# First attention: the mask is added by TensorE, the maxima are plain reductions, and VectorE copies the second head's row of maxima

## The chip, the cores and the metric

The kernel runs on one core of a Trainium2 chip. The metric is device time in microseconds (us) of one launch. TensorE (matmuls, PE in the profile; its weight loads are PEld), VectorE (DVE), ScalarE (ACT), GpSimd (POOL) and SyncE (SP, which issues the DMAs here) each work through a list of their own, and wait for each other by semaphores.

## The reference, cut to what matters

The input is x with 4 batches of 512 rows of 256. The first layer is `x + LN(attn(LN(x)))`, the second has an attention with 16 heads of 128 and a mixture of experts. The change lies in the first attention, which has 16 heads of 16 dimensions:

```python
sim = jnp.einsum('bhsd,bhtd->bhst', q, k) * scale
causal = jnp.tril(jnp.ones((S, S), dtype=bool))
sim = jnp.where(causal[None, None], sim, -jnp.inf)
weights = jax.nn.softmax(sim, axis=-1)
out = jnp.einsum('bhst,bhtd->bhsd', weights, v)
```

## The kernel before, in words

**Stages.** The first 58 us load, normalise and project x. Then the first attention runs in `step1(s)` on TensorE, VectorE, ScalarE and GpSimd, for 32 pairs of heads, s = 0 to 31, one pair in a step; its last step ends near 229 us. After it all engines meet at a fence (`meet`), and the second attention, the shared experts, the routed experts and a last sum follow.

**One pair of heads.** Head 0 of a pair (a = 0) has its queries and keys in partitions 0 to 63 of the tile `stk`, head 1 in partitions 64 to 127. A matmul of one head uses 64 rows of the array. The scores are made twice. In the first pass (`score`, line 1610) the queries are the rows of PSUM, and only the part that the causal mask keeps is computed: for the query block n (1 to 4) 128 x 128n scores. VectorE takes the negated maximum of each row (`row_max`, `mask_and_max`, line 1135): one custom instruction that negates the scores, adds the mask and keeps the minimum, and an accumulator read that writes the result to a column of `least`. TensorE transposes `least` (line 1653, which calls `turn`, line 1574) into a bank, in which row 0 and row 64 now hold the maxima of the two heads. ScalarE copies these two rows, 1 x 512 each, to `stk` (lines 866 to 868). The second pass (`score_t`, line 1617) makes the transposed scores with this row as one more term of the sum, so that the maximum is subtracted by the matmul itself, and ScalarE takes the exponential (`exp`, line 862). GpSimd zeroes what the mask forbids there, and `values` (line 1627) multiplies by v.

**The order of a step on TensorE** (line 1604 on). It is written out by hand, and the pairs overlap: while pair s is in its second pass, pair r = s + 1 is in its first.
1. `S1_PARTS` of pair r: the scores (0, 4), (1, 4) and (0, 2), written as (head, n), in banks 0, 1 and 2. Each waits for the maxima that still use its bank, those of pair s of the "rest".
2. The transposes of `least` of pair s. They wait for all maxima of s (`a1_max`) and for the third exponential of pair s - 1, whose bank they take.
3. `values` of the first key block of pair s - 1, and in odd steps the transposes of `o1_sum`.
4. `S1_REST` of pair r: (0, 3), (1, 3), (0, 1), (1, 1), then (1, 2). (0, 3) waits for the maximum (0, 4), (1, 3) for the maximum (1, 4), and (1, 2) for the maximum (0, 2).
5. After the wait for ScalarE's copies (`a1_m`, line 1686) the first three `score_t` of pair s.
6. The other `values`, and other work by step number (the output projection in steps s % 8 = 2 takes most).
7. `score_t` (1, 2), (0, 3), (1, 3), (0, 1), (1, 1); (0, 3) and (1, 3) wait for the first and second exponential.

**VectorE** takes in a step the maxima (0, 4), (1, 4), (0, 2) of pair s + 1, in odd steps `weigh` (line 1186), then the maxima (0, 3), (0, 1), (1, 3), (1, 1), (1, 2), and at some steps the statistics and scalings of the layer's end. **ScalarE** takes the two copies, exponentials 0 and 1, in even steps a copy of `o1_sum`, then exponentials 2 to 4, and at some steps copies of the layer's end. Below a step is counted from the start of its transposes of `least` to the next such start.

The last stage (lines 1492 to 1506) takes statistics of the final sums, with a semaphore `t_st` of its own.

## Time and profile before

| | |
|---|---|
| median of 3 runs | 1226.99 us (1226.29 to 1227.85) |
| the profiled execution | 1226.03 us |
| its span in the profile | 1224.3 us |
| granted TensorE clock, mean | 0.987 of full speed |
| 32 steps of the first attention | 57.9 to about 229 us |

The profile lists instructions by engine and by the line that issued them. Its durations go from the start of an instruction to its last result, so that instructions of one engine overlap, and two that follow each other start closer together than their durations say.

### The profile page before, as it was taken

To read this page: it belongs to the slowest core of one execution; us is meant where nothing else is said; L and a number is where in the kernel's file an instruction comes from. 1 tells how busy PE (TensorE), PEld (TensorE's weight loads), DVE (VectorE), ACT (ScalarE), POOL (GpSimd) and SP (SyncE) were. 2 spreads that over 40 slices of the span, in tenths; PEclk is the share of its full clock that TensorE was granted. 3 is DMA by queue.
4 is the path that set the end of the run, shared out by engine and by line. 5 is a ranking of instruction groups with operands and counts; after the bars stand their busy time and mean duration, and the time that the engine had idled before them with its cause. 6 is when DMAs were issued, how large, how long until landed. Compare 5 with 4: busy or idle time off the path is not lost.

```text
span 1224.3 us, 25085 instructions
## 1 busy us (share of the span) xinstructions
PE 1167.3 (95%) x7980; PEld 1004.5 (82%) x7980; DVE 895.2 (73%) x2799; ACT 692.3 (57%) x1717; POOL 580.1 (47%) x844
## 2 busy tenths in 40 slices
PE   6999999899999999999999999999998889999994
PEld 5766566689999999999999999999997769999961
DVE  5777888577777777887777887778876755555555
ACT  3487888655556565556564565655566434444432
POOL 4063655454344444447353365534354446666650
PEclk9999999999999999999999999999999989999998
DMA  8965655355631121212112132111214137777776
GB/s 264 286 184 170 178 164 176 91 178 175 204 109 62 57 84 57 80 52 91 68 36 69 36 102 73 43 63 35 70 62 134 61 114 122 117 119 118 111 143 206
DMA packets 111715, 139.58 MB, mean 114 GB/s; under 512 B 11300, under 2 KB 94756, under 8 KB 111460
## 3 DMA queue, kind: packets, MB, share of 16 engines
q1 hardware_dynamic: 97140, 119.10, 32.1%
q0 software_dynamic: 14448, 18.88, 9.6%
q8 instruction: 69, 1.13, 0.4%
q14 instruction: 58, 0.48, 0.1%
HBM read 63.36 MB, written 61.87 MB: 102 GB/s over the span
## 4 chain that ended last, share of the span: by engine, by line
PE 79%; DVE 6%; ACT 3%; POOL 3%; issue 3%; DMA 3%; SPq 2%; POOLq 0%; ACTq 0%; DVEq 0%
PE bank L1513 59%; PE bank L1755 6%; PE bank L1932 4%; PE bank L1574 2%; PE bank L1627 2%; PE bank L1610 2%; PE bank L1617 1%; POOL xs_rows L704 1%; DMA sum_rows<-mid,goal 1%; POOL sum_rows L766 1%; PE bank L1911 1%; PE bank L1942 1%; SPq L393 1%; DVE bank L1135 1%; ACT pT L862 1%
## 5 line engine op out<-in xcount | busy, mean ns | idle before, releaser
L1135 DVE CUSTOM_DVE_ANT_0 bank<-bank,mask 128x512 f32<-128x512 f32 (+3 forms) x512 | 235.3, 522 | 40.4 <-PE bank L1610 20.4
L970 ACT ACTIVATE p<-bank,stat 128x512 f32<-128x512 f32 (+3 forms) x256 | 131.4, 526 | 137.9 <-issue 133.2
L557 POOL CAST w_hl<-raw_qkv 128x512 fp32r<-128x512 f32 x96 | 58.5, 610 | 313.3 <-DMA raw_qkv<-in_qkvo 159.6
L1513 PE MATMUL bank<-xT,w_hl 128*128 128x512 f32 x768 | 189.6, 395 | 0.0
L1513 PEld LDWEIGHTS bank<-xT,w_hl 128*128 128x128 f32 x768 | 144.1, 188 | 34.6
L766 POOL DMA_INDIRECT sum_rows<-mid,goal x79 | 123.1, 1559 | 75.4 <-DVE mid L1468 64.3
L1513 PE MATMUL bank<-pT,v 128*128 128x128 f32 (+3 forms) x768 | 137.3, 328 | 0.0
L1234 DVE SCALAR_TENSOR_TENSOR qk<-bank,qk 128x512 fp32r<-128x512 f32 x128 | 87.1, 688 | 66.8 <-ACT qk L910 66.5
L1513 PE MATMUL bank<-qk 128*128 128x512 f32 (+3 forms) x768 | 130.8, 320 | 3.1 <-DVE pT L1345 2.4
L1513 PEld LDWEIGHTS bank<-qk 128*128 128x128 f32 x768 | 120.6, 191 | 12.2 <-DVE v L1234 2.6
L558 POOL TENSOR_TENSOR w_hl<-raw_qkv,w_hl 128x512 fp32r<-128x512 f32 x96 | 124.0, 1292 | 7.8
L910 ACT ACTIVATE qk<-bank 128x512 fp32r<-128x512 f32 x128 | 76.1, 596 | 78.4 <-PE bank L1513 77.9
L1513 PEld LDWEIGHTS bank<-pT,v 128*128 128x128 f32 x768 | 109.7, 190 | 2.9
L1513 PE MATMUL bank<-wo_hl,o 128*128 128x256 f32 x768 | 107.6, 290 | 1.8 <-DVE o L1387 1.4
L1345 DVE TENSOR_TENSOR pT<-bank,pT 128x128 fp32r<-128x128 f32 (+3 forms) x256 | 107.0, 480 | 0.0
L1360 DVE SCALAR_TENSOR_TENSOR hs<-bank,part,hs 128x256 f32<-128x256 f32 x256 | 105.8, 474 | 1.1 <-PE bank L1513 1.1
L1513 PEld LDWEIGHTS bank<-w_hl,xT 128*128 128x128 f32 x768 | 99.3, 188 | 5.7
L1513 PE MATMUL bank<-w_hl,xT 128*128 128x256 f32 x768 | 101.1, 280 | 0.0
L1513 PE MATMUL bank<-w_hi,sh_hi 128*128 x316 | 97.5, 350 | 1.3 <-issue 1.2
L1513 PEld LDWEIGHTS bank<-wo_hl,o 128*128 128x128 f32 x768 | 95.9, 191 | 2.4 <-DVE o L1387 1.8
L862 ACT ACTIVATE pT<-bank 128x512 f32<-128x512 f32 x160 | 85.3, 604 | 19.6 <-PE bank L1617 18.2
L960 ACT ACTIVATE pT<-bank 128x128 fp32r<-128x128 f32 (+3 forms) x256 | 91.1, 453 | 0.0
(237 smaller groups left out, 2284.6 us busy)
## 6 DMA issues: line engine op xcount, KB each, us to landing
raw_qkv<-in_qkvo SPq DMA_DIRECT2D x32, 768.0 KB, 5.6
xs_rows<-blank SPq DMA_DIRECT2D x32, 520.0 KB, 3.5
xs_rows<-blank SPq DMA_DIRECT2D x5, 2730.0 KB, 14.0
xrow<-xs_rows SPq DMA_DIRECT2D x79, 130.0 KB, 2.5
raw_o<-in_qkvo SPq DMA_DIRECT2D x32, 256.0 KB, 3.8
sum_rows<-blank SPq DMA_DIRECT2D x3, 2176.0 KB, 8.5
stk<-xT SPq DMA_DIRECT2D x96, 64.0 KB
stk<-k_hl SPq DMA_DIRECT2D x96, 64.0 KB
```

Of the source, the lines that this page charges most:

```text
L558: pool.tensor_tensor(lo, raw, f32(hi), ALU.subtract).then_inc(done, 1)
L766: pool.indirect_dma_start(sum_d[sum_of(i)], bass.IndirectOffsetOnAxis(goal[:, i % NY:i % NY + 1], 0), yt[:, i % NY, :], None, compute_op=A ...
L862: act.activation(pT1[:, s % 2, i, :], st1(s, i)[:, :], ACT.Exp).then_inc(a1_exp, 1)
L910: act.activation(dst, qkv_bank(n, i)[:, :], ACT.Copy, scale=(SCALE2 if i == 0 else 1.0))\
L960: act.activation(pT2[:, HI, QOFF[kj]:QOFF[kj + 1]], bank[t][:, 0:TB - P * kj], ACT.Copy).then_inc(b_pth, 1)
L970: act.activation(p2[:, n % 2, POFF[qi]:POFF[qi + 1]], s2(t), ACT.Exp, scale=-1.0, bias=stat2[:, 0, n % 2, t:t + 1], accum_out=stat2[:, 1, ...
L1135: return dve.tensor_tensor_reduce(scores, scores, mask[:, TB - scores.shape[1]:], scale=-1.0, scalar=-2.0 * MASKED, op0=ALU.add, op1=ALU.m ...
L1234: dve.scalar_tensor_tensor(lo, qkv_bank(n, i)[:, :], SCALE2 if i == 0 else 1.0, f32(hi), ALU.mult, ALU.subtract).then_inc(b_lo, 1)
L1345: dve.tensor_tensor(pT2[:, LO, QOFF[kj]:QOFF[kj + 1]], bank[t][:, 0:TB - P * kj], f32(pT2[:, HI, QOFF[kj]:QOFF[kj + 1]]), ALU.subtract).th ...
L1360: ins = dve.scalar_tensor_tensor(own, bank[4 + c][:, D * (j - 2 * c):D * (j - 2 * c + 1)], part2[:, n % 4, TPB - 1 - j:TPB - j], own, ALU. ...
L1513: ins = pe.matmul(out, a, b, start=start and i == 0, stop=stop and i == len(pairs) - 1, **kw)
L1755: ins = pe.transpose(bank[t][:, P * (qi - kj):P * (qi - kj + 1)], p2[:, (n - 1) % 2, POFF[qi] + P * kj:POFF[qi] + P * (kj + 1)], ident[:, :])
```

## The change

The additions to the first attention are: `ident16`, an identity in bf16; `forbid`, a matmul of this identity with the mask, accumulated onto the last 128 columns of a score block (of the blocks n = 3 and n = 1 of a head together, 256 columns); and a semaphore `a1_md`. `row_max` becomes a `tensor_reduce` with the maximum, positive instead of negated, so that the row of ones in `stk` becomes a row of -1. VectorE copies row 64 to `stk` between its first maximum (0, 4) and its second (1, 4); ScalarE copies row 0 alone. The second attention keeps its custom instruction. In the last stage the semaphore `t_st` goes, and `link`, which waits for each pair of statistics, takes its place.

```diff
--- before.py
+++ after.py
@@ -87,6 +87,7 @@
         xT = sb(ctx, "xT", [P, B, 2, C, TB], F32R)
         ident = sb(ctx, "ident", [P, P])
 
+        ident16 = sb(ctx, "ident16", [P, P], BF16)
         mask = sb(ctx, "mask", [P, TB], BF16)
         ln_w = sb(ctx, "ln_w", [P, 2, C])
         gate_raw = sb(ctx, "gate_raw", [P, C, E])
@@ -216,7 +217,7 @@
 
         stk_in = [sem(f"stk_in{i}") for i in range(NSTK)]; stk_zero = sem("stk_zero")
         a1_zero = sem("a1_zero"); a1_vpad = sem("a1_vpad"); a1_s = sem("a1_s"); a1_max = sem("a1_max")
-        a1_mt = sem("a1_mt"); a1_m = sem("a1_m"); a1_st = sem("a1_st"); a1_exp = sem("a1_exp"); a1_sel = sem("a1_sel")
+        a1_mt = sem("a1_mt"); a1_m = sem("a1_m"); a1_md = sem("a1_md"); a1_st = sem("a1_st"); a1_exp = sem("a1_exp"); a1_sel = sem("a1_sel")
         a1_pv = sem("a1_pv"); a1_oe = sem("a1_oe"); a1_ot = sem("a1_ot")
         a1_xo = sem("a1_xo"); a1_xt = sem("a1_xt"); a1_o = sem("a1_o")
 
@@ -250,7 +251,7 @@
         e_h = sem("e_h"); e_ht = sem("e_ht"); e_htc = sem("e_htc"); e_dn = sem("e_dn"); e_y = sem("e_y")
         y_sent = [sem(f"y_sent{i}") for i in range(NY)]
 
-        t_in = [sem(f"t_in{i}") for i in range(2 * B)]; t_sum = sem("t_sum"); t_old = sem("t_old"); t_st = sem("t_st"); t_mean = sem("t_mean")
+        t_in = [sem(f"t_in{i}") for i in range(2 * B)]; t_sum = sem("t_sum"); t_old = sem("t_old"); t_mean = sem("t_mean")
         t_x = sem("t_x"); t_out = sem("t_out")
         stored = sem("stored")
 
@@ -505,7 +506,8 @@
                                base=0, pattern=[[-1, P]], channel_multiplier=1).then_inc(const, 1)
             pool.wait_ge(const, 4)
             pool.tensor_copy(mask[:, :], mask_f).then_inc(const, 1)
-            pool.wait_ge(const, 5)
+            pool.tensor_copy(ident16[:, :], ident[:, :]).then_inc(const, 1)
+            pool.wait_ge(const, 6)
             pool.memset(blank[:, :], 0.0).then_inc(d_blank, 1)
             pool.wait_ge(d_blank, 1)
             pool.iota(blank[:, D:D + 1].bitcast(I32), [[0, 1]], base=NOWHERE, channel_multiplier=0)\
@@ -513,7 +515,7 @@
             pool.memset(f32(stk[:, :, :, :]), 0.0).then_inc(stk_zero, 1)
             for a in range(2):
                 pool.wait_ge(stk_zero, 1 + a)
-                pool.memset(f32(stk[64 * a:64 * a + 1, :, 1, :]), 1.0).then_inc(stk_zero, 1)
+                pool.memset(f32(stk[64 * a:64 * a + 1, :, 1, :]), -1.0).then_inc(stk_zero, 1)
             pool.wait_ge(stk_zero, 3)
             pool.wait_ge(ph1_wl, 1)
             pool.tensor_tensor(qkv1_hl[:, LO, :, 2 * D:3 * D], qkv1[:, :, 2 * D:3 * D],
@@ -863,9 +865,7 @@
 
                 if s < N1:
                     act.wait_ge(a1_mt, s + 1)
-                    for a in range(2):
-                        act.activation(stk[64 * a:64 * a + 1, s % NSTK, 0, :], st1(s, 0)[64 * a:64 * a + 1, :], ACT.Copy)\
-                           .then_inc(a1_m, 1)
+                    act.activation(stk[0:1, s % NSTK, 0, :], st1(s, 0)[0:1, :], ACT.Copy).then_inc(a1_m, 1)
                 if s >= 6 and s % 8 == 6:
                     take_oT((s - 6) // 4)
                 if b >= 0 and k == 2:
@@ -1180,7 +1180,7 @@
                 def row_max(a, *sizes):
 
                     for n in sizes:
-                        ins = mask_and_max(s1(a, n), least[:, (s + 1) % 2, n - 1, 64 * a:64 * a + 1])
+                        ins = dve.tensor_reduce(least[:, (s + 1) % 2, n - 1, 64 * a:64 * a + 1], s1(a, n), AX.X, ALU.max)
                     ins.then_inc(a1_max, 1)
 
                 def weigh(i):
@@ -1200,8 +1200,14 @@
                 if s + 1 < N1:
                     if s >= 1:
                         dve.wait_ge(a1_mt, s)
-                    for i, (a, n) in enumerate(S1_PARTS):
-                        dve.wait_ge(a1_s, 6 * (s + 1) + i + 1)
+                    dve.wait_ge(a1_s, 6 * (s + 1) + 1)
+                    row_max(0, TPB)
+                if 0 <= s < N1:
+                    dve.wait_ge(a1_mt, s + 1)
+                    dve.tensor_copy(stk[64:65, s % NSTK, 0, :], st1(s, 0)[64:65, :]).then_inc(a1_md, 1)
+                if s + 1 < N1:
+                    for i, (a, n) in enumerate(S1_PARTS[1:]):
+                        dve.wait_ge(a1_s, 6 * (s + 1) + i + 2)
                         row_max(a, n)
                 if s >= 3 and s % 2 == 1:
                     weigh((s - 3) // 2)
@@ -1493,10 +1499,8 @@
                 tiles = slice(TPB * b, TPB * (b + 1))
                 for half in range(2):
                     dve.wait_ge(t_sum, 2 * b + half + 1)
-                    for j in range(2):
-                        ins = dve.bn_stats(st6[:, TPB * b + 2 * half + j, :], sums(b, half)[:, D * j:D * (j + 1)])
-                        ins.then_inc(t_st, 1)
-                dve.wait_ge(t_st, TPB * (b + 1))
+                    link(*[dve.bn_stats(st6[:, TPB * b + 2 * half + j, :], sums(b, half)[:, D * j:D * (j + 1)])
+                           for j in range(2)])
                 ask_root(tiles)
                 if b:
                     finish(b - 1)
@@ -1513,7 +1517,7 @@
                     ins = pe.matmul(out, a, b, start=start and i == 0, stop=stop and i == len(pairs) - 1, **kw)
                 return ins
 
-            pe.wait_ge(const, 5)
+            pe.wait_ge(const, 6)
             def turn_x(b):
                 pe.wait_ge(ph1_xn, b * TPB + TPB)
                 if b:
@@ -1524,6 +1528,13 @@
                                            ident[:, :])
                     ins.then_inc(ph1_tp, 1)
 
+            def forbid(a, *sizes):
+
+                own = s1(a, sizes[0])[:, P * (sizes[0] - 1):P * sizes[0]] if len(sizes) == 1 else \
+                    bank[a][:, 2 * P:4 * P].rearrange("p (i n) -> p i n", i=2)
+                future = mask[:, TB - P:] if len(sizes) == 1 else mask[:, TB - P:].unsqueeze(1).to_broadcast([P, 2, P])
+                return pe.matmul(own, ident16[:, :], future, start=False, stop=True, skip_group_check=True)
+
             def first_scores():
 
                 pe.wait_ge(stk_in[0], 16 * 7)
@@ -1532,7 +1543,8 @@
                         pe.wait_ge(ph1_lo, 4 * (B - 1) + 1)
                     rows = slice(64 * a, 64 * a + 64)
                     pe.matmul(s1(a, n), stk[rows, 0, 0, P * (n - 1):P * n], stk[rows, 0, 1, 0:P * n],
-                              start=True, stop=True).then_inc(a1_s, 1)
+                              start=True, stop=False, skip_group_check=True)
+                    forbid(a, n).then_inc(a1_s, 1)
 
             turn_x(0)
             for b in range(B):
@@ -1608,7 +1620,7 @@
 
                     rows, m, qi = slice(64 * a, 64 * a + 64), r % NSTK, n - 1
                     return pe.matmul(s1(a, n), stk[rows, m, 0, P * qi:P * (qi + 1)], stk[rows, m, 1, 0:P * n],
-                                     start=True, stop=True)
+                                     start=n > 1, stop=False, skip_group_check=True)
 
                 def score_t(a, n):
 
@@ -1634,7 +1646,8 @@
                     pe.wait_ge(stk_in[r % NSTK], 16 * 7 * (r // NSTK + 1))
                     for i, (a, n) in enumerate(S1_PARTS):
                         pe.wait_ge(a1_max, 6 * (r - 1) + i + 4)
-                        score(r, a, n).then_inc(a1_s, 1)
+                        score(r, a, n)
+                        forbid(a, n).then_inc(a1_s, 1)
                 if 0 <= s < N1:
 
                     if s >= 1:
@@ -1677,13 +1690,15 @@
                     for a, n in S1_REST:
                         if n == 3:
                             pe.wait_ge(a1_max, 6 * r + 1 + a)
-                        ins = score(r, a, n)
+                        score(r, a, n)
                         if n == 1:
-                            ins.then_inc(a1_s, 1)
+                            forbid(a, 3, 1).then_inc(a1_s, 1)
                     pe.wait_ge(a1_max, 6 * r + 3)
-                    score(r, 1, 2).then_inc(a1_s, 1)
+                    score(r, 1, 2)
+                    forbid(1, 2).then_inc(a1_s, 1)
                 if 0 <= s < N1:
-                    pe.wait_ge(a1_m, 2 * (s + 1))
+                    pe.wait_ge(a1_m, s + 1)
+                    pe.wait_ge(a1_md, s + 1)
                     for i, (a, n) in enumerate(S1_PARTS):
                         if s >= 1 and i:
                             pe.wait_ge(a1_exp, 5 * (s - 1) + i + 3)
```

## Rows read from the trace of the kernel before

**Rows 1.** The page, busy us (share of the span) and instructions of each engine
```profile
PE 1167.3 (95%) x7980; PEld 1004.5 (82%) x7980; DVE 895.2 (73%) x2799; ACT 692.3 (57%) x1717; POOL 580.1 (47%) x844
```

**Rows 2.** Stretches of eight steps: us, PE PEld DVE ACT POOL busy, clock, DMA, GB/s
```profile
57.90:97.30 39.40, 38.37 (x373) 23.77 (x372) 32.22 (x141) 31.10 (x60) 21.18 (x45) 0.91 0.65 197
97.30:140.70 43.40, 41.92 (x425) 26.40 (x424) 36.23 (x163) 34.64 (x67) 22.16 (x68) 1.00 0.58 169
140.70:185.50 44.80, 43.21 (x434) 27.12 (x433) 38.20 (x167) 37.04 (x71) 25.84 (x79) 1.00 0.60 175
185.50:229.00 43.50, 41.69 (x424) 26.57 (x424) 34.06 (x150) 36.69 (x70) 25.39 (x77) 1.00 0.43 128
```

**Rows 3.** Timeline of even step 4: start, us, engine line op out<-in xcount [idle before]
```profile
78.09 0.66 PE L1574 MATMUL bank<-ident,least 128*128 128x128 f32 x4
...
78.24 0.73 DVE L1135 CUSTOM_DVE_ANT_0 bank<-bank,mask 128x512 f32<-128x512 f32 x1
...
78.89 0.14 DVE L1135 DVE_READ_ACCUMULATOR2_ANT least<- 128x1 f32 x1
...
78.79 1.20 ACT L867 ACTIVATE stk<-bank 1x512 fp32r<-1x512 f32 x2 [0.28 <-PE bank L1574]
...
79.25 0.67 PE L1610 MATMUL bank<-stk 64*128 64x384 f32 x5
...
80.04 0.62 PE L1617 MATMUL bank<-stk 64*128 64x512 f32 x3
...
80.58 1.09 ACT L862 ACTIVATE pT<-bank 128x512 f32<-128x512 f32 x2 [0.59 <-PE bank L1617]
...
82.03 1.60 ACT L862 ACTIVATE pT<-bank 128x512 f32<-128x512 f32 x3
...
82.70 0.66 PE L1574 MATMUL bank<-ident,least 128*128 128x128 f32 x4 [0.20 <-ACT pT L862]
```

**Rows 4.** Timeline of odd step 3, which ends at 78.09
```profile
73.15 0.66 PE L1574 MATMUL bank<-ident,least 128*128 128x128 f32 x4 [0.20 <-ACT pT L862]
...
75.71 2.80 ACT L862 ACTIVATE pT<-bank 128x512 f32<-128x512 f32 x5 [0.62 <-PE bank L1617]
...
77.59 0.14 DVE L1135 DVE_READ_ACCUMULATOR2_ANT least<- 128x1 f32 x1
...
77.78 0.18 PEld L1610 LDWEIGHTS bank<-stk 64*128 64x128 f32 x1 [0.20 <-DVE least L1135]
```

**Rows 5.** Groups by shape, 62 to 230 us: xcount | busy, mean ns | idle before
```profile
L1135 DVE CUSTOM_DVE_ANT_0 bank<-bank,mask 128x512 f32<-128x512 f32 x60 | 40.4, 714 | 9.6 <-PE bank L1610 9.5
...
L1135 DVE CUSTOM_DVE_ANT_0 bank<-bank,mask 128x128 f32<-128x128 f32 x60 | 19.8, 330 | 0.0
...
L1135 DVE DVE_READ_ACCUMULATOR2_ANT least<- 128x1 f32 x240 | 33.6, 140 | 0.0
...
L867 ACT ACTIVATE stk<-bank 1x512 fp32r<-1x512 f32 x62 | 36.1, 583 | 4.0 <-PE bank L1574 3.0
```

**Rows 6.** Line 1258: durations in ns, minimum/median/maximum, first and last start
```profile
L1258 DVE TENSOR_REDUCE lg<-bank x4: 261/262/281, 481.4 to 945.5; 128x64 f32<-128x128 f32 x4
```

**Rows 7.** TensorE streams and loads: second attention, line 1610, and a bf16 load
```profile
243.26 3.01 PE L1513 MATMUL bank<-xT,w_hl 128*128 128x512 f32 x12
...
246.11 1.58 PE L1513 MATMUL bank<-w_hl,xT 128*128 128x256 f32 x12
...
144.88 0.61 PE L1610 MATMUL bank<-stk 64*128 64x512 f32 x3
...
L1744 PEld LDWEIGHTS bank<-msk,earlier x4: 96/98/99, 523.0 to 962.3; 128*128 128x128 bf16 x4
```

**Rows 8.** Timeline of the start of the kernel, GpSimd and the first transposes
```profile
2.32 0.61 POOL L507 CAST mask<-xn_mid 128x512 bf16<-128x512 f32 x1
...
9.88 1.94 PE L1523 MATMUL bank<-ident,xn 128*128 128x128 f32 x8 [9.88 <-DVE xn L1104]
```

**Rows 9.** Timeline of the last stage, VectorE statistics at line 1497
```profile
1202.66 0.76 DVE L1497 BATCH_NORM_STATS2 st<-bank 128x6 f32<-128x256 f32 x2 [1.96 <-PE bank L1513]
```

## The prediction

> **What bounds the kernel now.** The page comes first: TensorE is busy for 95% of the span, VectorE for 73% and ScalarE for 57% [rows 1]. That is a mean over stages. The change touches the first attention, so I cut that into stretches of eight steps: 39.4, 43.4, 44.8 and 43.5 us, 5.35 us for a step on average [rows 2]. TensorE's share stays above 95% there, but its weight loads fill only about 60%, and its gaps are waits. So what bounds a step must be read from the order of events in one.
>
> An even step without other work lasts 82.70 - 78.09 = 4.61 us [rows 3]. Count from its transposes, at 0. They take 0.66, and ScalarE's two copies run from 0.70 to 1.90; the rest of the next pair's scores starts at 1.16 and is issued by then; the second pass starts at 1.95, the exponentials at 2.49, and the next transposes wait for the third exponential (the releaser in brackets is ACT). Here the two serial copies are on the path. VectorE isn't: its second maximum begins at 0.15 and its third at 0.80.
>
> An odd step lasts 78.09 - 73.15 = 4.94 us [rows 4]. Its five exponentials take 2.80 from 75.71, and as two take 1.09 where one takes 0.60 [rows 3], each adds 0.49: the third ends at 77.53, early. What comes last is VectorE's fifth maximum of the rest (the read at 77.59 ends at 77.73, TensorE's load follows at 77.78). So even steps end by ScalarE, odd ones by VectorE, each with little in reserve on the other path.
>
> **The change part by part.**
>
> *One copy less on ScalarE.* It frees 0.58 us a step [rows 5]. Alone it would let the second pass of an even step start near 1.37 if nothing else were late.
>
> *The other copy goes to VectorE, ahead of the maximum (1, 4).* This is the step that decides. VectorE can't start it before the transposes are done, at 0.70, and now the maxima (1, 4) and (0, 2) stand behind it. Before, they began at 0.15 and 0.80, while ScalarE copied. TensorE's list has the scores (1, 3), waiting for the maximum (1, 4), ahead of the second pass. The second pass therefore starts after this sum: 0.70, the copy, the maximum (1, 4), a hand-over of 0.05 (77.73 to 77.78 [rows 4]), and the rest of the scores from (1, 3) on.
>
> The copy of 1x512 on VectorE isn't in the trace. ScalarE's takes 0.58, and the longest VectorE instruction on 512 elements adds 0.65 (78.24 to 78.89) and lasts 0.71 [rows 3, 5]. I take 0.62, ends 0.58 and 0.71.
>
> *Plain maxima.* A reduction of 128 elements from PSUM lasts 0.262 [rows 6], the custom instruction 0.330 for 128 and 0.714 for 512, which is 1.00 ns an element, and it has a read of 0.140 behind it [rows 5]. A reduction of 512 is then 0.262 + 384 x 1.00 = 0.65; its ends are 0.26 (as for 128) and 0.85 (custom plus read). I take 0.65. Eight maxima save some 0.06 each, 0.5 a step, on VectorE.
>
> *Six mask matmuls a step.* The stream costs 3.01 / 12 / 512 = 0.49 ns a column [rows 7]. From (1, 3) on the rest now has 384 + 256 (mask) + 128 + 256 (mask) + 256 + 128 (mask) = 1,408 columns, 0.69 us. The sum is 0.70 + 0.62 + 0.65 + 0.05 + 0.69 = 2.71, against 1.95: the second pass starts 0.76 later in an even step. In the odd one it started 0.54 ahead of the first exponential, as in the even one, so at 75.17 or 2.02: 0.69 later. The new wait for VectorE's copy (`a1_md`) ends at 1.4 and is no wait by then.
>
> The three scores at the head of a step get masks too. Before, those of the two heads share the array: 512 + 512 + 256 columns take 0.61 with the last one's latency [rows 7], where 1,280 columns one after another are 0.63 without it. So before it is 768 columns, 0.38; after, a full-height mask stands between the heads, and it is 1,664 columns, 0.82: 0.44 more, just ahead of the transposes. Ends: 0.10 (three masks at 128 columns each, half hidden) and 0.60.
>
> *How a step ends then.* Even: the second exponential ends at 81.67 [rows 3], plus 0.76 is 82.43; plus a hand-over of 0.05, 0.34 for the last second-pass scores (512 columns of one head and half a load of 0.18 [rows 4]), and 0.77 of the 0.82 (the last mask runs beside the transposes' load) gives 83.59, against 82.70: +0.89 (by ScalarE's path it would be +0.76). Odd: it ends at 75.71 + 1.09 = 76.80, plus 0.69, 0.05, 0.34 and 0.77 gives 78.65, against 78.09: +0.56. VectorE's own chain: the copy adds 0.62 and the waits for TensorE some 0.3, the reductions give back 0.5; it ends about 0.1 later than now and isn't last.
>
> Ten steps are even ones with no or little other work: 8.9 us. Four are odd ones with none: 2.2. The other 17 have work of the layer's end on VectorE, TensorE or ScalarE; their slack takes a part, and I put them at 0.43, the odd value less a quarter: 7.3. Sum 18.4 us. Nothing of it is hidden later, since all engines meet at a fence after the stage. SyncE's loads of `stk` wait for the second pass of an earlier pair; they move with the steps and gain room.
>
> *The rest.* The cast of the identity on GpSimd is in front of TensorE's first wait: at most 0.61 (the cast of four times the size), which ends at 2.93; the memsets behind it feed transfers that start only after the first projections; and TensorE's first work waits for VectorE until 9.88 [rows 8]; without that cover it would cost those 0.61. Three masks in the first scores: 0.2 at most. In the last stage VectorE waits 1.96 for the sums of a half [rows 9], so that the wait in `link` lies in a wait; 0, within 0.2 either way.
>
> So the profiled execution's 1226.03 (span 1224.3) becomes 1244.4. The median of the runs is 1.0 above it; I say **1244 us**.
>
> **A rule against the trace.** The loads of full-height weights run beside matmuls here: the transposes' loads are among 0.66 for four of them [rows 3]. The Trainium skill, "TensorE: Matmul & The Clock Gate", section "The mechanism", says that a weight load overlaps running matmuls only when they use different row groups. By that rule no load of the identity, and no score's load behind it, would be hidden; this is rival C below. The same skill, "VectorE: DVE Perf Modes", section "Two Vector instructions with no wait between them", says that an instruction whose output or input starts in another group of 32 partitions waits for all earlier ones to finish. By it the copy from partition 64, and the maximum behind it, would overlap nothing, some 0.1 a step more, 3 us in all; no row shows it.
>
> **The rivals.**
>
> A. *Faster*. The even steps end by ScalarE, and one of its two copies goes. If VectorE were through with copy and maximum (1, 4) by the time TensorE has to start the rest so as not to be late, the 16 even steps would win up to 0.58 each: 1217 us. The point from which it decides: 0.70 + copy + maximum + 0.05 + 0.69 below 1.95, so copy and maximum together below 0.51 us. For it: VectorE has time over (73% busy). Against: the copy alone is at least 0.58 by any row. Chance 0.04.
>
> B. *No difference*. The low ends together: copy 0.58, maximum 0.26, masks beside the streams (0.38 for the rest) give 1.97, and the masks at the head fall in waits. Then 1226 to 1228. Against: the maximum can't well take as long for 512 elements as for 128. Chance 0.05. The same masks with a maximum of 0.65 give a second pass at 2.40, +0.45 in an even step and +0.38 in an odd one: 13 us, 1239, inside the range.
>
> C. *Loads exposed*. Each mask costs its own load, 0.10, and the load of the scores behind it, 0.18 [rows 4, 7]. Three masks on the path of the rest are then 0.84 a step more, in 31 steps 26 us: 1270. Half of this is 1257. For it: nothing in the trace has a full-height load between half-height ones. Against: the transposes above. Chance 0.08 for the whole.
>
> D. *VectorE becomes the bound*. Odd steps end by it now. If the reductions cost as much as before (0.85 for 512), nothing is given back, and its chain is longer by the copy and the waits, 0.62 + 0.3. With the later second pass both kinds of step then come to about +0.9, 28 us: 1254. Chance 0.13.
>
> The forecast, the order of TensorE's list with sizes about as taken: chance 0.70.
>
> **How the numbers follow.** The range takes in B's half case below and D and half of C above: 1232 to 1258. What is left out is A, B and C, 0.17. About 0.2% (2.5 us) is what a measurement can tell from no change. Faster by more: A, 0.04. Within: B, 0.05. Slower: the rest, 0.91.
>
> **What would show it.** Right: in an even step without other work, the copy on VectorE starts 0.7 after the transposes and the second maximum begins after it, near 1.3; the first matmul of the second pass starts at 2.6 to 2.8; ScalarE is idle before its exponentials by over 1 us instead of 0.59; the stretches of eight steps grow by 4 to 6 us each; everything behind the fence lasts as long as before. Wrong: a second pass that starts at 2.0 or earlier; reductions of 512 elements that last under 0.4 or over 0.8; the three head scores and their masks within 0.5 us; or a lower granted clock in the stage, which I have at the level of now.

## The result, and the profile after

The kernel became slower: a median of 1315.07 us in 4 runs (1308.44 to 1327.08) against 1226.64 us, a ratio of 1.0735, 95% interval 1.0694 to 1.0776. The forecast was 1244, with a range up to 1258. The profiled execution after the change has a span of 1317.3 us, 93.0 more than before.

The page of the changed kernel answers to [rows 1]; from it the busy line, the TensorE clock in 40 slices of 33 us, and the chain by engine:

```profile
PE 1259.3 (96%) x8172; PEld 1048.7 (80%) x8172; DVE 910.2 (69%) x2575; ACT 675.9 (51%) x1685; POOL 580.9 (44%) x845
...
PEclk9957988799999999999999999999999998999998
...
PE 86%; DVE 5%; issue 2%; POOL 2%; DMA 2%; ACT 1%; SPq 1%; POOLq 0%; DVEq 0%; ACTq 0%
```

The clock line is the surprise: slices at 5, 7 and 8 tenths between the third and the eighth, which is the first attention. The stretches of seven or eight steps, with the columns of [rows 2], say the same:

```profile
59.40:126.30 66.90, 65.39 (x364) 35.46 (x364) 31.28 (x71) 24.34 (x46) 19.46 (x41) 0.59 0.36 110
126.30:188.00 61.70, 60.00 (x473) 34.85 (x474) 39.57 (x106) 30.61 (x59) 20.38 (x59) 0.94 0.41 122
188.00:251.80 63.80, 62.67 (x483) 36.72 (x483) 41.67 (x110) 33.10 (x63) 26.84 (x83) 0.91 0.41 120
251.80:314.80 63.00, 61.60 (x475) 36.29 (x474) 41.15 (x109) 31.81 (x61) 24.66 (x75) 0.91 0.30 88
```

The first seven steps ran at a mean of 0.59 of the full clock, the others at 0.91 to 0.94. Before it was 1.00 in all stretches but the first [rows 2]. From the first transposes of `least` to the last the stage takes 314.8 - 59.4 = 255.4 us, where it took 166.5 before; of the 93.0 us all but some 4 lie there.

The timeline of one odd step at full clock (126.28 to 133.26, 6.98 us) answers to [rows 3] and [rows 4]. In it line 1586 is the transposes, 1622 the scores of the first pass, 1536 the masks, 1629 the second pass, 1207 VectorE's copy, 1183 the reductions:

```profile
126.28 0.61 PE L1586 MATMUL bank<-ident,least 128*128 128x128 f32 x4
...
126.93 0.69 DVE L1207 CAST stk<-bank 1x512 fp32r<-1x512 f32 x1 [0.74 <-PE bank L1586]
...
127.65 1.02 DVE L1183 TENSOR_REDUCE least<-bank 128x1 f32<-128x512 f32 x2
...
128.39 0.19 PEld L1622 LDWEIGHTS bank<-stk 64*128 64x128 f32 x2 [0.23 <-DVE least L1183]
...
128.76 0.10 PEld L1536 LDWEIGHTS bank<-mask,ident 128*128 128x128 bf16 x1 [0.19 <-issue]
...
128.98 0.18 PEld L1622 LDWEIGHTS bank<-stk 64*128 64x128 f32 x1
...
129.23 0.10 PEld L1536 LDWEIGHTS bank<-mask,ident 128*128 128x128 bf16 x1
...
129.45 0.18 PEld L1622 LDWEIGHTS bank<-stk 64*128 64x128 f32 x1
...
129.76 0.10 PEld L1536 LDWEIGHTS bank<-mask,ident 128*128 128x128 bf16 x1
...
129.92 0.29 PEld L1629 LDWEIGHTS bank<-stk 64*128 64x128 f32 x3
...
130.45 2.79 ACT L864 ACTIVATE pT<-bank 128x512 f32<-128x512 f32 x5 [2.94 <-PE bank L1629]
...
131.75 0.44 PE L1622 MATMUL bank<-stk 64*128 64x512 f32 x1
...
132.12 0.10 PEld L1536 LDWEIGHTS bank<-mask,ident 128*128 128x128 bf16 x1 [0.24 <-issue]
...
132.28 0.18 PEld L1622 LDWEIGHTS bank<-stk 64*128 64x128 f32 x1
...
132.71 0.10 PEld L1536 LDWEIGHTS bank<-mask,ident 128*128 128x128 bf16 x1 [0.25 <-issue]
...
132.88 0.18 PEld L1622 LDWEIGHTS bank<-stk 64*128 64x128 f32 x1
...
133.19 0.10 PEld L1536 LDWEIGHTS bank<-mask,ident 128*128 128x128 bf16 x1
...
133.26 0.28 PE L1586 MATMUL bank<-ident,least 128*128 128x128 f32 x1
```

The reader is to see four things, from the transposes at 0 (126.28). VectorE's copy starts at 0.65 and the maximum behind it 0.72 later. The score (1, 3) is loaded at 2.11. From there to the second pass (129.92) are 1.53 us, and each load of a mask or of a score behind a mask starts only after a gap. The block at the head of a step, from 131.75 to the transposes' first load at about 133.20, takes 1.45.

### The profile page after: what moved, and what is told of

It reads as the page before. It is cut to its first block, busy times and chain, and to the rows that moved or that the text cites. A ratio compares the mean times of both kernels' runs of the same rounds, so it can differ in the third digit from the quotient of the medians.

```text
span 1317.3 us, 25250 instructions
## 1 busy us (share of the span) xinstructions
PE 1259.3 (96%) x8172; PEld 1048.7 (80%) x8172; DVE 910.2 (69%) x2575; ACT 675.9 (51%) x1685; POOL 580.9 (44%) x845
## 4 chain that ended last, share of the span: by engine, by line
PE 86%; DVE 5%; issue 2%; POOL 2%; DMA 2%; ACT 1%; SPq 1%; POOLq 0%; DVEq 0%; ACTq 0%
PE bank L1517 55%; PE bank L1622 5%; PE bank L1770 5%; PE bank L1947 5%; PE bank L1639 4%; PE bank L1536 3%; PE bank L1586 3%; PE bank L1629 3%; PE bank L1926 1%; POOL xs_rows L706 1%; PE bank L1957 1%; DMA sum_rows<-mid,goal 1%; DVE xn L1104 1%; DVE x_sb L1495 0%; DVE least L1183 0%
## 5 line engine op out<-in xcount | busy, mean ns | idle before, releaser
L1183 DVE TENSOR_REDUCE least<-bank 128x1 f32<-128x256 f32 (+3 forms) x256 | 111.2, 485 | 62.6 <-PE bank L1536 61.5
L864 ACT ACTIVATE pT<-bank 128x512 f32<-128x512 f32 x160 | 85.1, 601 | 98.4 <-PE bank L1629 97.6
L1135 DVE CUSTOM_DVE_ANT_0 bank<-bank,mask 128x512 f32<-128x512 f32 (+3 forms) x256 | 118.1, 524 | 19.1 <-PE bank L1517 19.1
L546 POOL TENSOR_SCALAR_AFFINE_SELECT pT<-pT 128x256 f32<-128x256 f32 x128 | 51.7, 406 | 159.5 <-ACT pT L864 154.8
L1622 PE MATMUL bank<-stk 64*128 64x384 f32 (+1 forms) x253 | 99.2, 451 | 5.4 <-DVE least L1183 5.4
```

The source lines that it names most:

```text
L864: act.activation(pT1[:, s % 2, i, :], st1(s, i)[:, :], ACT.Exp).then_inc(a1_exp, 1)
L1135: return dve.tensor_tensor_reduce(scores, scores, mask[:, TB - scores.shape[1]:], scale=-1.0, scalar=-2.0 * MASKED, op0=ALU.add, op1=ALU.m ...
L1183: ins = dve.tensor_reduce(least[:, (s + 1) % 2, n - 1, 64 * a:64 * a + 1], s1(a, n), AX.X, ALU.max)
L1622: return pe.matmul(s1(a, n), stk[rows, m, 0, P * qi:P * (qi + 1)], stk[rows, m, 1, 0:P * n], start=n > 1, stop=False, skip_group_check=True)
```

## The experiments

The expectations name three theories. Theory 1 was formed from the timeline above: TensorE lets the array run empty at each change between 64-row and 128-row matmuls. Rival 2: any additional matmuls in these places cost this. Rival 3: the copy on VectorE is the cause. "Height" is the number of rows of the array that a matmul uses: 64 for the scores of one head, 128 for the masks and the transposes. All kernels but half_height, half_act, no_masks, plain_max and late_copy apply the whole mask ahead of the maximum; these five take some maxima over future keys too, which only shifts both sides of the softmax.

**half_height**: the same masks, in the 64 rows of their own head.

```diff
-                future = mask[:, TB - P:] if len(sizes) == 1 else mask[:, TB - P:].unsqueeze(1)...
-                return pe.matmul(own, ident16[:, :], future, start=False, stop=True, ...)
+                rows = slice(64 * a, 64 * a + 64)
+                future = mask[rows, TB - P:] if len(sizes) == 1 else mask[rows, TB - P:].unsqueeze(1)...
+                return pe.matmul(own, ident16[rows, :], future, start=False, stop=True, ...)
```

> The six mask matmuls of a step stay, with the same columns and places, but each takes 64 rows of the array, those of its own head (so it masks half of the queries; the other half takes its maximum over future keys too, which the softmax cancels). Theory 1, the cost is the change between half-height and full-height work, at which TensorE lets the array run empty: the stretch from the load of score (1, 3) to the second pass falls from 1.53 us to about 0.8, the block at the head of a step from 1.45 to about 0.9, steps without other work to 5.3 to 5.7 us, the time to 1235 to 1255. Rival 2, any twelve more TensorE instructions in these places cost this: steps stay near 7 us, the time above 1290. Rival 3, the copy on VectorE is the cause: no change, 1305 to 1325.

Measured: 1246.0 us, ratio 1.0163 (1.0086 to 1.024), clock 0.983. The same two places in its timeline (line numbers one higher: 1623 scores, 1537 masks, 1630 second pass, 1587 transposes):

```profile
105.71 0.29 PEld L1623 LDWEIGHTS bank<-stk 64*128 64x128 f32 x3 [0.82 <-DVE least L1183]
...
105.88 0.26 PEld L1537 LDWEIGHTS bank<-mask,ident 64*128 64x128 bf16 x2
...
106.05 0.20 PEld L1623 LDWEIGHTS bank<-stk 64*128 64x128 f32 x1
...
106.12 0.29 PEld L1630 LDWEIGHTS bank<-stk 64*128 64x128 f32 x2
...
106.65 1.09 ACT L864 ACTIVATE pT<-bank 128x512 f32<-128x512 f32 x2 [1.82 <-PE bank L1630]
...
107.95 0.45 PE L1623 MATMUL bank<-stk 64*128 64x512 f32 x1
...
108.41 0.30 PE L1537 MATMUL bank<-mask,ident 64*128 64x128 bf16 x2
...
108.83 0.31 PEld L1587 LDWEIGHTS bank<-ident,least 128*128 128x128 f32 x3 [0.25 <-ACT pT L864]
```

From the load of (1, 3) at 105.71 to the second pass at 106.12 it takes 0.41 us instead of 1.53; 0.8 was expected. From the first head score at 107.95 the last two masks begin at 108.41, and the transposes at 108.83 wait for the exponential again. Steps without other work last 5.28 and 5.24 us instead of 6.97. The number, the columns and the places of the masks are the same; only the height differs. Rival 2 falls here, and most of rival 3. Two things come with the height and are not separated here: the change itself, and that the two heads' matmuls can run beside each other in the array.

**no_masks**: the changed kernel without the masks.

```diff
-                        score(r, a, n)
-                        forbid(a, n).then_inc(a1_s, 1)
+                        score(r, a, n).then_inc(a1_s, 1)
```

> The changed kernel without any mask matmul (the maxima are taken over the whole blocks, future keys among them). Theory 1: only the copy on VectorE and the plain reductions are left; the second pass starts at about 2.6 us of a step, steps without other work last 5.0 to 5.3, the time is 1230 to 1245, and the granted clock is back at 0.98 or more. Rival 3, the copy is the cause: 1290 or more. Rival 2 expects as theory 1.

Measured: 1241.09 us, ratio 1.0123 (1.0077 to 1.0169). Steps without other work last 5.22 and 5.17. So the copy and the reductions cost 14 us. The half-height masks cost about 5 more by the medians and 3.1 by the stage as profiled (183.1 against 180.0 us); the intervals of the two ratios overlap, so that a cost of the half-height masks is not clear of the noise.

**act_copies**: both copies on ScalarE, masks as in the changed kernel.

```diff
-                    act.activation(stk[0:1, s % NSTK, 0, :], st1(s, 0)[0:1, :], ACT.Copy).then_inc(a1_m, 1)
+                    for a in range(2):
+                        act.activation(stk[64 * a:64 * a + 1, s % NSTK, 0, :], st1(s, 0)[64 * a:64 * a + 1, :], ACT.Copy)\
+                           .then_inc(a1_m, 1)
-                    dve.wait_ge(a1_mt, s + 1)
-                    dve.tensor_copy(stk[64:65, s % NSTK, 0, :], st1(s, 0)[64:65, :]).then_inc(a1_md, 1)
```

> The changed kernel with both copies on ScalarE again, VectorE makes none; masks and reductions stay. Theory 1: the masks keep the block of the rest and the head block long; the second pass starts 0.4 to 0.7 earlier in a step, the time falls by 10 to 25 us to 1285 to 1305, and the clock stays below 0.98. Rival 3: the time falls to 1235 or less.

Measured: 1278.12 us, ratio 1.0425 (1.0275 to 1.0575), below the stated 1285. It is the middle of two executions that lie apart: 1270.74 us with a mean clock of 0.990, which is the profiled one, and 1285.51 with 0.977. The expectation that the clock stays below 0.98 was met by one of them. In the profiled one steps without other work last 6.04 (even) and 6.62 (odd), and the stage's window (same columns as above) has the clock at full:

```profile
58.70:268.80 210.10, 209.38 (x1790) 125.18 (x1790) 128.76 (x365) 138.07 (x258) 91.42 (x256) 1.00 0.45 134
```

So the masks without the copy cost 44 us at full clock (1270.74 against 1227.01; the stage grew from 166.5 to 210.1). Against the changed kernel's profiled stage of 255.4 us this is 45.3 less, more than the copy costs by itself in any run.

**copy_only**: the kernel before, with the copy of the second head on VectorE behind its first maximum.

```diff
+                    row_max(0, TPB)
+                if 0 <= s < N1:
+                    dve.wait_ge(a1_mt, s + 1)
+                    dve.tensor_copy(stk[64:65, s % NSTK, 0, :], st1(s, 0)[64:65, :]).then_inc(a1_md, 1)
```

> The kernel before with only the second head's copy moved to VectorE, between the maxima (0, 4) and (1, 4) (the custom instruction with its mask stays; the last stage's wait as in the changed kernel, for want of a semaphore). Theory 1: VectorE is late with the maximum (1, 4) by 1.3 us, the second pass starts at about 2.6 to 2.8 instead of 1.95, steps grow by 0.4 to 0.7, the time is 1236 to 1248. Rival 3: 1290 or more. No cost at all: 1226.

Measured: 1252.98 us, ratio 1.022 (1.0149 to 1.029), a little above the stated range. Steps without other work last 5.40 and 5.57. With the custom instruction the copy costs 26 us, with plain reductions (no_masks) 14. So the shorter reductions give back up to a half once VectorE is on the path: 0.18 us in an even step and 0.40 in an odd one. A part of the 12 us is the clock's, which was at half for 17.1 us of this run's stage and for 10.2 of no_masks'.

**grouped**: the full-height masks behind one another.

```diff
                         score(r, a, n)
-                        forbid(a, n).then_inc(a1_s, 1)
+                    for a, n in S1_PARTS:
+                        forbid(a, n).then_inc(a1_s, 1)
```

The rest is changed in the same way: the five scores, then their three masks.

> The changed kernel with the same six full-height masks, but behind one another: the three scores at the head of a step first, then their three masks, next to the full-height transposes; the five scores of the rest first, then their three masks. Changes between half and full height fall from about eleven to three a step. Theory 1 (each change costs about 0.15 us): 1.0 to 1.4 us less in a step without other work, so 5.6 to 6.0 instead of 6.97, the time 1255 to 1285. If each full-height mask itself cost it, wherever it stands: near 7 us and above 1300.

Measured: 1265.78 us, ratio 1.0322 (1.0299 to 1.0344). The rest in its timeline:

```profile
135.23 0.52 PEld L1622 LDWEIGHTS bank<-stk 64*128 64x128 f32 x4 [0.81 <-DVE least L1183]
...
135.88 0.22 PEld L1536 LDWEIGHTS bank<-mask,ident 128*128 128x128 bf16 x3
...
136.26 0.29 PEld L1629 LDWEIGHTS bank<-stk 64*128 64x128 f32 x3 [0.16 <-issue]
```

1.03 us from the load of (1, 3) to the second pass instead of 1.53, with the same instructions; of the steps without other work the even ones last 6.02 for the most part (5.84 to 6.24) and the odd ones 5.84 to 5.85. Around the masks eleven changes of height a step became three, and 6.97 became 5.93 on average: 0.13 us a change. In this figure is what the scores of the two heads give back by standing side by side again; the run doesn't separate it. The same price comes out of the changed kernel's own step, if its streams are put at one after another, as the prediction had them: (1.53 - 0.69) / 6 = 0.14 and (1.45 - 0.82) / 5 = 0.13.

**two_halves**: the whole mask in two half-height matmuls.

```diff
+                for one, future in ((ident16[rows, :], mask[rows, TB - P:]), (earlier[rows, :], ones[rows, :])):
+                    future = future if len(sizes) == 1 else future.unsqueeze(1).to_broadcast([64, 2, P])
+                    ins = pe.matmul(own, one, future, start=False, stop=True, skip_group_check=True)
```

The tiles `earlier` and `ones` hold the identity and the mask of the other 64 queries until the fence.

> The whole mask, as in the changed kernel, but each mask matmul is made of two of 64 rows, both in the rows of their own head (the second with the identity and the mask of the other 64 queries, in two tiles that are idle in this stage). Twelve mask matmuls a step, no change of height for them. Theory 1: the streams alone, 0.05 to 0.15 us a step more than with one half: steps without other work 5.3 to 5.5, 1246 to 1256. If the number of mask matmuls cost: above 1300.

Measured: 1253.67 us, ratio 1.0223 (1.0198 to 1.0248), steps of 5.44 and 5.32. Twelve mask matmuls instead of six, the same mask on the scores, and 61 us less than the changed kernel.

**plain_max**: no masks, both copies on ScalarE; the edits of no_masks and act_copies together.

> No masks and both copies on ScalarE: the kernel before, with plain reductions in place of the custom instruction (and a sign turned). Theory 1: even steps stay at 4.6, where ScalarE ends them; odd ones, which VectorE ended at 4.94, lose 0.1 to 0.3; the time is 1218 to 1226, a little below before. If the custom instruction was no part of any path: 1226 to 1228.

Measured: 1225.66 us, ratio 0.9997 (0.9984 to 1.001) in 10 runs. Odd steps without other work fell from 4.94 to 4.67, as theory 1 has it, but nothing is left of it in the time: some steps at the batches' ends became longer (5.96 and 6.68 in one profile, against 4.69 and 5.20). The granted clock was at half for 3.4 us in the second of these two (187.9 to 191.3); why the first is longer is open. As profiled the whole stage is 1.5 us shorter than before, 165.0 against 166.5, which the medians don't show.

**late_copy**: no masks, VectorE's copy behind three maxima instead of one.

```diff
-                    dve.wait_ge(a1_mt, s + 1)
-                    dve.tensor_copy(stk[64:65, s % NSTK, 0, :], st1(s, 0)[64:65, :]).then_inc(a1_md, 1)
                 if s + 1 < N1:
                     for i, (a, n) in enumerate(S1_PARTS[1:]):
...
+                if 0 <= s < N1:
+                    dve.wait_ge(a1_mt, s + 1)
+                    dve.tensor_copy(stk[64:65, s % NSTK, 0, :], st1(s, 0)[64:65, :]).then_inc(a1_md, 1)
```

> The kernel without masks, VectorE's copy behind its maxima (0, 4), (1, 4) and (0, 2) instead of behind the first. Theory 1, it is the place of the copy in VectorE's list that costs: the copy ends near 2.0 us of a step, the second pass starts at 2.0 to 2.2 instead of 2.6, steps fall from 5.2 to 4.7 to 4.9, the time is 1224 to 1232. If the copy's own length on VectorE costs: 1238 to 1242 as without masks.

Measured: 1230.47 us, ratio 1.0042 (1.0027 to 1.0058), and steps without other work of mostly 4.65 to 4.76 (even) and 4.93 (odd). The same copy on the same engine, 10.6 us less than in no_masks: its place in VectorE's list was the cost, as the prediction had it.

**half_act**: half-height masks and both copies on ScalarE.

> The half-height masks of half_height, and both copies on ScalarE: with half_height, act_copies and the changed kernel the fourth corner of the square of copy and height. Theory 1: half-height masks cost their streams and the sharing, the copy costs nothing, so steps of 4.6 to 4.9 us and 1226 to 1234. Rival: masks of any height disturb the order of ScalarE and VectorE without the copy as well: 1240 or more.

Measured: 1228.06 us, ratio 1.0011 (0.9991 to 1.0031). With this the square is full: 1228.1 with neither, 1246.0 with the copy (+17.9), 1278.1 with the full-height masks (+50.1), and 1315.1 with both, 19 us above the sum of the parts, 1296.1. These are medians over executions with different clocks. By the stage as profiled the corners are 164.9, 183.1 and 210.1 us, and 228.3 for the changed kernel once its steps are put at the lengths that they have at full clock (the sum is explained in the next section). There the parts add up: 164.9 + 18.2 + 45.2 = 228.3. Nothing is left over for copy and height together but the clock.

**changed_again** and **busy_array** ask whether it is the clock. The first is the changed kernel unaltered; the second gives TensorE work where it waits:

```diff
-                    values(s - 1, TPB)
+                    for _ in range(3):
+                        values(s - 1, TPB)
```

> The changed kernel itself once more, beside the next two. Its first four executions had mean clocks of 0.948 to 0.970 and times of 1327 to 1308 us, in that order. Expected: again 1305 to 1330 with a clock of 0.94 to 0.975, with a long stretch at half clock at the start of the stage, and steps without other work of 6.97 us wherever the clock is full.

> The changed kernel with the eight value matmuls behind the transposes done three times instead of once (the same result, started anew each time), at a place where TensorE waits for VectorE's copy and maximum until 2.1 us of a step: 0.5 us more work of TensorE a step, little of it on the path. If the low clock comes from TensorE being too little at work between the masks: the clock is 0.975 or more, and the time falls in spite of the added work, to 1285 to 1302. If the clock doesn't go by that: 0.94 to 0.97 as before, and 1308 to 1335.

Measured, on the same chip, two executions each: 1322.56 us with a clock of 0.953 in both for the kernel unaltered, 1308.73 us with 0.987 and 0.982 for the one with more work (1305.42 to 1312.05; the ratios to before are 1.0794, 1.0752 to 1.0836, and 1.0682, 1.0605 to 1.0758). The windows of busy_array:

```profile
59.00:126.00 67.00, 65.81 (x596) 37.69 (x595) 38.79 (x92) 30.12 (x57) 22.61 (x49) 0.92 0.45 137
126.00:310.00 184.00, 183.52 (x1777) 111.20 (x1781) 116.63 (x311) 93.13 (x178) 75.17 (x231) 1.00 0.35 103
```

After 126 us its clock is full throughout, although its steps without other work are as long as the changed kernel's or longer (6.98 and 7.48). It lies above the 1285 to 1302 that were stated, since the added work lengthened the odd steps by 0.5 us. But with more work it took 14 us less. The two intervals touch, and one earlier execution of the unaltered kernel took 1308.44 us, so the time alone is weak evidence. The clock is not: the six executions of the unaltered kernel have 0.948 to 0.970, these two 0.982 and 0.987. The unaltered kernel's stage has 84.4 us at half clock (91.4 in changed_again), the one with more work 10.2.

## Why the prediction was wrong

**The step that failed is the price of the masks.** The prediction took 0.49 ns a column for their stream and nothing for the change between 64 and 128 rows: 0.69 us from (1, 3) on, and 0.82 for the block at the head. Measured are 1.53 and 1.45. Over the stage it priced the masks at some 5 us (18.4, less the 13 of its own case with the masks beside the streams), and at full clock they cost 48.3 (228.3 less the 180.0 of no_masks). The half-height run shows that masks of 64 rows cost less than was put down (0.41 for the block), so that the excess hangs on the height. The grouped run shows that it goes by the number of changes. The traces don't show the array's state itself; that it runs empty first is the reading of the gaps.

**The trace of before had rows of this cost, and the prediction didn't read them.** In 57 to 230 us its list of waits has, as total, times and longest:

```profile
PEld bank L1627 <- issue: 13.0, 61, 0.4
...
PEld bank L1574 <- issue: 8.8, 25, 0.4
```

Each is 0.2 to 0.4 us in which nothing releases TensorE. The height alone doesn't sort these waits. Line 1627 loads for the value matmuls, whose weights are 128 rows by 32 columns: 30 of its 61 waits come behind the 64-row second pass (0.26 us on average), but 31 come behind the transposes, which have 128 rows too (0.17). Of the 25 waits of line 1574, the transposes, 24 come behind value matmuls, 128 rows behind 128 rows (0.35). So what these rows show is a wait wherever the rows or the columns of the weights change. One step of before has three of them in a row:

```profile
135.31 0.42 PEld L1574 LDWEIGHTS bank<-ident,least 128*128 128x128 f32 x4 [0.51 <-ACT pT L862]
...
135.90 0.16 PEld L1627 LDWEIGHTS bank<-pT,v_pad 128*32 128x32 f32 x8 [0.17 <-issue]
...
136.47 0.42 PEld L1574 LDWEIGHTS bank<-ident,o_sum 128*128 128x128 f32 x4 [0.41 <-issue]
...
137.05 0.18 PEld L1610 LDWEIGHTS bank<-stk 64*128 64x128 f32 x1 [0.17 <-issue]
```

The last of them is a change of height alone, from 128 x 128 to 64 x 128. The changed kernel has the same kind of wait at the masks, 100 times:

```profile
PEld bank L1536 <- issue: 26.4, 100, 0.4
...
ACT pT L864 <- PE bank L1629: 97.6, 37, 4.7
```

**The evidence used against it was of another kind.** The prediction set the four transposes' loads, full height behind full height, against the Trainium skill's rule ("TensorE: Matmul & The Clock Gate", section "The mechanism") that a load overlaps running matmuls only when the row groups differ. In the changed kernel the transposes' load still follows a mask at once (133.19 to 133.20; both are 128 x 128), and loads between different heights don't. Read as a rule on a full-height load between half-height matmuls, it agrees with the trace: a mask's load at 132.12 begins 0.37 after the score at 131.75. As a general rule on full-height loads it doesn't. Rival C carried it and priced 0.84 us a step on the rest, the very difference between 1.53 and 0.69. But it left out the head of the step, 0.6 more, and had a chance of 0.08.

**The granted clock was the second failure.** It was named as what would make the forecast wrong, and wasn't priced. Steps of 6.97 us at full clock last 10.35 at half clock. Summing the 31 steps with the lengths that steps of their kind have at full clock (6.97 without other work, 7.39 and 9.70 with it, for example) gives 228.3 us for the stage's 31 intervals, against 255.4 as profiled: 27.1 us are the clock's. The share differs from execution to execution: 1308.4 us came with a mean clock of 0.970, 1327.1 with 0.948. A slip of 1 us stands beside this: 1244.4 was for the profiled execution, and with the 1.0 that the median lies above it the prediction's sum is 1245.4.

**The other steps held.**
- The copy on VectorE starts at 0.65, lasts 0.69 (forecast 0.62), and a reduction of 512 lasts 0.69 (0.65), of 128 0.28 (0.26). The maxima (1, 4) and (0, 2) stood behind the copy as said, and (1, 3) came at 2.11 against 2.02. These rows are from the stretch at full clock, grouped by shape (xcount | busy, mean ns | idle before):

```profile
L1183 DVE TENSOR_REDUCE least<-bank 128x1 f32<-128x512 f32 x15 | 10.3, 689 | 10.3 <-PE bank L1536 10.0
...
L1183 DVE TENSOR_REDUCE least<-bank 128x1 f32<-128x128 f32 x15 | 4.2, 281 | 0.0
...
L1207 DVE CAST stk<-bank 1x512 fp32r<-1x512 f32 x7 | 4.8, 689 | 4.5 <-PE bank L1586 4.5
```

- The second pass starts at 3.64, against the 2.71 forecast: 0.09 by copy and reduction, 0.84 by the rest. The step ends at 6.98 against 5.50, 1.48 later; these two and the head's 0.63 make 1.56, so that closes to 0.1.
- ScalarE waited for TensorE over 1 us in a step: 97.6 us in 37 waits.
- VectorE's chain wasn't last; rivals A, B and D fall.
- In place of the forecast sum of 18.4 us stand, from the stage's intervals of 166.5 (before), 180.0 (no_masks), 183.1 (half_height), 228.3 (changed, at full clock) and 255.4: copy and reductions 13.5, masks of half height 3.1 (for half of the queries; 8.6 for all, two_halves with 188.6), full instead of half height 45.2, clock 27.1; together 88.9. Without the last two the stage grows by 16.6, or 22.1 with the whole mask, against 18.4. The 13.5 meets the 13 that the prediction had for copy and reductions alone; that the masks' part comes near as well is partly luck, since it was priced for full-height streams one after another.
- From the last transposes of `least` to the end the time is 1002.5 us against 999.9; plain_max, with the same last stage as the changed kernel, has 1001.0. It was put at 0. The other runs have 1000.2 to 1006.1, so the 2.6 are not told from what executions differ by.

What stays open: what in TensorE's activity lowers the clock, how much of the full-height masks' price is the change and how much the lost running side by side, and why plain_max gains nothing in spite of shorter odd steps. No version that was run beats the kernel before.

## What to carry to other kernels

Where two heads share the array by row tiles, a matmul of another height between them isn't priced by its columns: each change cost about 0.13 us here, the lost sharing included, so keep the height (split the matmul into the rows of its tile) or put all of one height behind one another. Read the idle time before weight loads that the profile gives to "issue": here it marked the places where the rows or columns of the weights change, and such a change is paid already. When an instruction moves to another engine, look at what stands behind it in that engine's list; the same copy cost 14 us behind the first maximum and 5 behind the third.

## What the runs showed of the hardware that wasn't expected

- The granted clock of TensorE fell to 0.50 (1.2 of 2.4 GHz) in the changed kernel for 54.6 us from the start of the stage, and four times later in it for 3.4 to 13.7 us; before it had one stretch of 6.8 us there. The other kernels' profiles have 0 to 17.1 us at half clock in the stage. The 0 is act_copies, with the same masks in steps of mostly 6.04 to 7.06 us; its other execution, not profiled, had a mean clock of 0.977 instead of 0.990. With more work in the waits (busy_array) the clock was 0.982 and 0.987 against 0.953. The PE row of the page shows none of this: it says 96% for the changed kernel.
- VectorE's copy from partition 64 held the next reduction until it was through: 0.72 us from start to start, where two reductions of 512 and 256 follow at 0.61 (127.65 to 128.26). This agrees with the Trainium skill, "VectorE: DVE Perf Modes", section "Two Vector instructions with no wait between them", and it cost the 0.1 a step that the prediction had set aside from it.
